# A decoder layer in which GpSimd computes the low halves of the out projection's weights in place of VectorE

## The reference

```
x = layernorm(x + attention(x))          # 16 query heads, 4 key/value heads of 128, rotary,
                                         # causal windows of 128 queries x 256 keys
x = layernorm(x + cross(x, ctx))         # softmax over ctx's own energies, applied to x
x = layernorm(x + moe(x))                # 2 shared and 16 routed experts, top 4, width 176

# the end of attention, with out_kernel of shape (16 * 128, 256):
out = ob.reshape(b, t, H * D)
return jnp.dot(out, out_kernel)
```

## Time and profile before

| | |
|---|---|
| Median of three runs | 456.1 us (454.03 to 456.33) |
| Span of the profiled execution | 457.5 us, its own time beside the runs |
| PE (TensorE matmul) | 406.4 us busy, 89% |
| PEld (weight load) | 343.3 us, 75% |
| DVE (VectorE) | 308.9 us, 68% |
| ACT (ScalarE) | 267.0 us, 58% |
| POOL (GpSimd) | 168.3 us, 37% |
| Mean granted TensorE clock | 0.960 of full speed |

### The profile page before, as it was taken

The page is one execution under the profiler, slowest core; times in us unless marked ns, Lnnn a source line. Parts: engine busy times, 40 slices in busy tenths (PEclk is TensorE's granted clock), DMA queues, the critical chain, the costliest instruction groups (busy, mean ns, idle before and its releaser), DMA issues.

```text
span 457.5 us, 8275 instructions
## 1 busy us (share of the span) xinstructions
PE 406.4 (89%) x2297; PEld 343.3 (75%) x2297; DVE 308.9 (68%) x851; ACT 267.0 (58%) x659; POOL 168.3 (37%) x288
## 2 busy tenths in 40 slices
PE   3977898999889999899998896884899999999992
PEld 2766787999779988789997674561788888888871
DVE  1685999797987889887889745440655555555545
ACT  3566977785657775567774631610655555555553
POOL 0142656553664556535646402010222232222210
PEclk9986999999999999999999996997799999999997
DMA  6511230000000000000002950035433333333302
GB/s 225 198 47 47 91 116 25 3 0 2 1 1 23 0 0 0 0 0 0 0 0 60 327 183 0 0 44 99 113 92 95 100 96 91 96 100 94 90 10 92
DMA packets 20716, 29.29 MB, mean 64 GB/s; under 512 B 1305, under 2 KB 15794, under 8 KB 20696
## 3 DMA queue, kind: packets, MB, share of 16 engines
q1 hardware_dynamic: 20696, 29.05, 22.9%
HBM read 27.19 MB, written 1.86 MB: 63 GB/s over the span
## 4 chain that ended last, share of the span: by engine, by line
PE 67%; DVE 16%; issue 7%; DMA 4%; ACT 2%; POOL 2%; SPq 1%; POOLq 0%; DVEq 0%; ACTq 0%
PE bank L524 18%; PE bank L525 17%; PE bank L526 17%; PE bank L608 4%; PE bank L617 2%; PE bank L580 2%; PE bank L607 2%; DMA gates_d<-gatesT 2%; DMA gate_rows<-gates_d 1%; DVE by_sin L1047 1%; DVE by_cos L1046 1%; PE bank L574 1%; DVE scores L1057 1%; DVE xln L1118 1%; PE bank L680 1%
## 5 line engine op out<-in xcount | busy, mean ns | idle before, releaser
L1002 DVE TENSOR_TENSOR hid<-hid,gate_rows 128x512 f32<-128x512 f32 (+1 forms) x46 | 32.0, 699 | 68.8 <-ACT hid L810 50.8
L810 ACT ACTIVATE hid<-bank,b_cols 128x512 f32<-128x512 f32 (+1 forms) x50 | 34.3, 687 | 42.1 <-PE bank L526 42.1
L1286 POOL TENSOR_SCALAR nprobs<-probs,rsums 128x128 f32<-128x128 f32 x64 | 24.0, 375 | 91.6 <-DVE rsums L1064 86.2
L1293 POOL TENSOR_TENSOR w_lo<-w_raw,w_hi 128x256 fp32r<-128x256 f32 (+1 forms) x25 | 20.7, 829 | 89.6 <-ACT w_hi L802 89.6
L1278 POOL TENSOR_TENSOR queryT<-by_cos,by_sin 128x512 f32<-128x512 f32 x32 | 42.5, 1328 | 28.8 <-DVE by_sin L1047 27.8
L524 PE MATMUL bank<-hid_hi,w_hi 128*128 128x512 f32 (+1 forms) x100 | 40.1, 401 | 8.2 <-DVE hid_lo L989 8.0
L989 DVE TENSOR_TENSOR hid_lo<-hid,hid_hi 128x512 fp32r<-128x512 f32 (+1 forms) x50 | 39.3, 819 | 5.7 <-ACT hid_hi L819 3.1
L870 ACT COPY swapped<-bank 64x512 f32<-64x512 f32 x40 | 23.3, 583 | 32.6 <-PE bank L526 32.4
L524 PE MATMUL bank<-x2T_hi,w_hi 128*128 128x512 f32 (+1 forms) x100 | 40.5, 405 | 0.5 <-DVE xln L1031 0.5
L524 PE MATMUL bank<-xT_hi,wq_hi 128*128 128x256 f32 x128 | 38.8, 303 | 1.7 <-issue 1.2
L525 PE MATMUL bank<-x2T_lo,w_hi 128*128 128x512 f32 (+1 forms) x100 | 40.1, 401 | 0.0
(11 more groups left out here) (174 smaller groups left out, 1176.5 us busy)
## 6 DMA issues: line engine op xcount, KB each, us to landing
gate_rows<-gates_d SPq DMA_DIRECT2D x22, 512.0 KB
w_raw<-in_L_ffn_routed_w SPq DMA_DIRECT2D x2, 1408.0 KB, 8.2
w_raw<-in_L_ffn_routed_w SPq DMA_DIRECT2D x1, 2688.0 KB, 12.5
stage<-in_L_attn_q_kernel SPq DMA_DIRECT2D x4, 512.0 KB, 6.3
stage<-in_L_attn_out_kernel SPq DMA_DIRECT2D x4, 512.0 KB, 3.5
xb<-in_x SPq DMA_DIRECT2D x4, 256.0 KB, 2.9
res<-in_x SPq DMA_DIRECT2D x1, 1024.0 KB, 6.2
out<-x SPq DMA_DIRECT2D x8, 128.0 KB, 1.8
```

The costliest lines, as they stand in the source:

```text
L810: nc.scalar.activation(hid[0:n, par, h * HALF:(h + 1) * HALF], bank[2 + 2 * par + h][0:n, :], ACT.Relu, bias=b1_cols[0:n, bass.ds(c, 1)]). ...
L1002: nc.vector.tensor_tensor(hid[0:n, par, cols], hid[0:n, par, cols], gate_rows[0:n, par, cols], ALU.mult).then_inc(gated, 1)
L1286: nc.gpsimd.tensor_scalar(nprobs[:, u, 0:W], probs[:, u, 0:W], rsums[:, u, 0:1], 1.0, ALU.mult, ALU.mult)
```

## The change

`POOL_PIECES` names o0 to o3. `window_order` now gives GpSimd an order with the once-only work too: a piece of `POOL_PIECES` goes to GpSimd, the others stay on VectorE, all at the same places of `PIECE_AT`. GpSimd gets a function `once`, which waits for ScalarE's high half and subtracts, and signals a semaphore of its own, `w_lo_pool`. Those who waited for `w_lo` to count a piece of the out projection now wait for `w_lo_pool` (`project_out` on TensorE, the slot "y" on ScalarE, which keeps its wait for the others as well). The second branch of SyncE's wait is never taken: the last load, piece 9, waits for piece 5, which is VectorE's.

With the places of `PIECE_AT`, GpSimd's order in the first sequence becomes: normalise 6, o0, q5, normalise 7, q6, o1, normalise 8, normalise 9, o2, normalise 10, q7, normalise 11, o3, normalise 12.

```diff
@@ -108,6 +108,8 @@
 
 PIECE_NAMES = ["q0", "k", "q1", "q2", "v", "q3", "o0", "o1", "o2", "o3"]
 PIECE_AT = dict(zip(PIECE_NAMES, (-2.1, -2.05, -0.9, 2.2, 3.1, 5.4, 6.6, 8.1, 10.1, 12.1)))
+POOL_PIECES = PIECE_NAMES[6:]
+DVE_PIECES = 6
 ONCE_AT = {
     "pe": {"ctx turned": -2.4, "ctx projected": -2, "energy 0": -0.9, "energy 1": -0.85,
            "energy 2": 0.2, "energy 3": 0.25, "attT 0": 1.1, "attT 1": 1.15, "attT 2": 2.1,
@@ -137,8 +139,9 @@
     turns = [(in_window(at)[1], in_window(at)[0], work, of) for at, work, of in events]
     assert all(window in (0, 1) for _, window, _, _ in turns), engine
     turns += [(at, "once", name, 0) for name, at in ONCE_AT[engine].items()]
-    if engine in ("act", "dve"):
-        turns += [(at, "once", "piece", PIECE_NAMES.index(name)) for name, at in PIECE_AT.items()]
+    if engine != "pe":
+        turns += [(at, "once", "piece", PIECE_NAMES.index(name)) for name, at in PIECE_AT.items()
+                  if engine == "act" or (name in POOL_PIECES) == (engine == "pool")]
     return [(window, work, of) for _, window, work, of in sorted(turns, key=lambda e: e[0])]
 
 
@@ -338,7 +341,7 @@
         ld_ident, ld_tables, ld_res = sem("ld_ident"), sem("ld_tables"), sem("ld_res")
         ld_xb = sem("ld_xb")
         ld_stage = [sem(f"ld_stage{i}") for i in range(4)]
-        w_hi, w_lo = sem("w_hi"), sem("w_lo")
+        w_hi, w_lo, w_lo_pool = sem("w_hi"), sem("w_lo"), sem("w_lo_pool")
         projected, emptied = sem("projected"), sem("emptied")
         swap_done, rope_mul, rope_add = sem("swap_done"), sem("rope_mul"), sem("rope_add")
         split_hi = sem("split_hi")
@@ -452,7 +455,10 @@
             for n in range(4, len(PIECES)):
                 if n == 6:
                     small_loads()
-                sp.wait_ge(w_lo, n - 3)
+                if n - 4 < DVE_PIECES:
+                    sp.wait_ge(w_lo, n - 3)
+                else:
+                    sp.wait_ge(w_lo_pool, n - 3 - DVE_PIECES)
                 sp.dma_start(stage_view(n), PIECES[n][0]).then_inc(ld_stage[n % 4], 16)
             sp.dma_start(res[:], x_tiles).then_inc(ld_res, 16)
 
@@ -639,7 +645,7 @@
                     after("dve", "centT_lo")
                 if g == 0 and blk == 0:
                     e.wait_ge(res_done, b + 1)
-                e.wait_ge(w_lo, piece_count(f"o{g}"))
+                e.wait_ge(w_lo_pool, g + 1)
                 e.wait_ge(oT_done, pv_count(b, g, blk))
                 for a in range(G):
                     q = slice(a * W, (a + 1) * W)
@@ -850,7 +856,8 @@
                 if kind == "x":
                     nc.scalar.copy(xT_hi[:, j, :], o[:, 0:T]).then_inc(split_hi, 1)
                 elif kind == "y":
-                    e.wait_ge(w_lo, len(PIECES))
+                    e.wait_ge(w_lo, DVE_PIECES)
+                    e.wait_ge(w_lo_pool, len(PIECES) - DVE_PIECES)
                     e.sem_inc(act_passed, 1)
                     nc.scalar.copy(x2T_hi[:, :, bass.ds(b * T, T)],
                                    o[:].rearrange("p (k t) -> p k t", k=KC)).then_inc(x2_hi_done, 1)
@@ -1288,6 +1295,11 @@
                                         ALU.mult, ALU.mult).then_inc(norm_done, 1)
 
 
+            def once(_, n):
+                e.wait_ge(w_hi, n + 1)
+                nc.gpsimd.tensor_tensor(PIECES[n][2], stage_view(n), PIECES[n][1].bitcast(F32),
+                                        ALU.subtract).then_inc(w_lo_pool, 1)
+
             def low_w1(c, par, n=P):
                 e.wait_ge(w1_hi_done, c + 1)
                 nc.gpsimd.tensor_tensor(w1_lo[:, par, :, 0:n], w1_raw[:, :, bass.ds(c * P, n)],
@@ -1330,9 +1342,9 @@
 
             for s in (norm_done, turned):
                 e.sem_inc(s, AHEAD)
-            doers = {"slot": slot, "normalise": normalise, "norm 1": lambda b, _: layer_norm(b, 0),
+            doers = {"slot": slot, "normalise": normalise, "once": once, "norm 1": lambda b, _: layer_norm(b, 0),
                      "norm 2": lambda b, _: layer_norm(b, 1)}
-            take_turn("pool", 0, (0,), doers)
+            take_turn("pool", 0, (0, "once"), doers)
             with e.Fori(1, B) as b:
                 take_turn("pool", b, (0, 1), doers)
             take_turn("pool", B, (1,), doers)
```

## The result

The changed kernel took 459.98 us at the median of 18 runs (456.36 to 462.02), beside 456.38 for the kernel before on the same chip: a ratio of **1.0078, 95% interval [1.0055, 1.0100]**, 2.5 to 4.6 us slower. Two more sets of the same kernel gave 1.0059 [1.0025, 1.0094] and 1.0106 [1.0065, 1.0146]. The forecast was 457.0 and its likeliest case was "within 0.5%"; that was wrong.

The account below looks back on a forecast made before the run. VectorE looked limiting over 57 to 79 us, with TensorE's idle time capping any gain. Turn 8's +2.2 us less idle 0.84 and 0.45 gave +0.9 us on the 456.1 median: 457.0 us, range 454.3 to 460.4.

Parts of the forecast that it names:

- within 0.5%: Whole kernel: time changes by less than 2.3 us either way, chance 0.60.
- the ceiling: TensorE's listed idle, 57.5 to 79 us: even an infinitely fast VectorE gains at most about 1.6 us (1.57 idle).
- The cost of one subtraction: Each 128x1024 piece on GpSimd: 2.38 us, extrapolated from 256 and 512 columns; ends 1.26 and 2.92.
- GpSimd's queue: Ahead of TensorE's turn 8, first sequence: two pieces of 2.38 us delay normalise 8, making turn 8 2.2 us late.
- The holds: VectorE instructions behind a GpSimd piece wait for its end: by_sin 5 some 2.6 us, an ntop near 2 us.
- the replay: Instruction-by-instruction re-timing of the first sequence from 57.6 us; puts sequence 1's query product 0.9 us late, at 79.34.
- The tie: At o3: o3 (76.59) and ntop 13 (76.60) nearly coincide; if o3 wins, ntop 13 is held to 78.97; chance 0.22.
- The first rival: o3 holds ntop 13, so sequence 1's query product comes at 80.9 us; +2.5 us, 458.6 on the median, chance 0.22.
- rival 2: TensorE's granted clock falls behind 1.9 us idle ahead of turn 8; up to +4.3 us, 460.4 on the median, chance 0.18.
- The third rival: GpSimd's subtraction lets by_sin 5 through, so only GpSimd's own order counts; -1.2 us, 454.9 on the median, chance 0.18.
- the stated range: Whole kernel: total time predicted between 454.3 and 460.4 us.

Follow-up runs that it names:

- The version with two of the four pieces hidden: Kernel before, all pieces on VectorE, subtractions o0 and o1 moved early into VectorE's idle stretch at 40 to 44 us; ratio 0.9961.
- The run that writes without reading: Changed kernel with each GpSimd subtraction replaced by three zero fills of the low half, which read nothing; ratio 1.0015.
- halves: Changed kernel with each GpSimd subtraction split into two instructions of 512 columns; ratio 1.0036.
- o3 alone: Changed kernel with only subtraction o3 on GpSimd, o0 to o2 staying on VectorE; ratio 1.0035.

## Why the prediction was right and wrong

**What bounds the kernel, and the ceiling.** Right as a reading of place: the 3.8 us that the chain shows on wo_lo were no measure of the gain. But the ceiling was too low. The version with two of the four pieces hidden gained 1.74 us of distance, with 0.45 of the listed idle still there, where the ceiling had been 1.57 for all four. It had counted only the idle stretches that the records list, and these start at a matmul's modelled end. From start to start more was lost: behind the values product turn 7 came 0.57 us sooner in the version with two pieces early (0.28 listed), turn 10 another 1.00 behind turn 8 (0.84 listed).

**The cost of one subtraction.** Right. 2.38 us estimated, measured (the stage tile's GpSimd instruction, columns as in the earlier trace rows):

```profile
L1300 POOL TENSOR_TENSOR wo_lo<-stage,wo_hi x4: 2361/2386/2396, 57.9 to 75.7; 128x1024 fp32r<-128x1024 f32 x4
```

**GpSimd's queue and turn 8.** The size is right, the cause only in part. From the values product to turn 8 it is 10.71 us before (67.77 - 57.06) and 12.81 after (68.94 - 56.13): 2.1 us late, 2.2 predicted. The prediction called this GpSimd's queue, with two pieces in it. But behind o0 GpSimd stood idle, for by_sin 5 and for the reciprocal of head 7:

```profile
60.86 1.28 POOL L1285 TENSOR_TENSOR queryT<-by_cos,by_sin 128x512 f32<-128x512 f32 x1 [0.63 <-DVE by_sin L1054]
...
63.67 0.37 POOL L1293 TENSOR_SCALAR nprobs<-probs,rsums 128x128 f32<-128x128 f32 x1 [1.52 <-DVE rsums L1071]
```

That reciprocal, before and after:

```profile
63.07 0.15 DVE L1064 RECIPROCAL rsums<-psums 128x2 f32<-128x2 f32 x1
...
63.28 0.15 DVE L1071 RECIPROCAL rsums<-psums 128x2 f32<-128x2 f32 x1
```

It comes 6.01 us behind the values product before and 7.15 after. So 1.1 of the 2.1 us come by o0's hold of by_sin 5, through VectorE, and only the other 1.0 by o1 in GpSimd's own queue. The run that writes without reading agrees: with by_sin 5 free, turn 8 was sooner although the queue was longer. Later places agree too: the input transposes were forecast 20.70 us behind the values product and came 20.57 behind it (76.70 - 56.13).

**The holds.** Right in kind, and by_sin 5 in size (2.65 us; about 2.6 predicted). The Trainium skill (SBUF — State Buffer, "Who interferes with whom") says that the loser waits for the whole instruction, and that a VectorE instruction with two SBUF inputs meets only GpSimd instructions that read. Both agree with the runs: holds end with the GpSimd instruction, halves of 512 columns halve them, and behind a fill by_sin took 0.68 us. ntop 10 lasted less than expected (0.65 us, where the prediction looked for near 2), and by_sin 7 was hardly held (0.79 us), since o1 and o2 were nearly over.

**A wait that the replay missed.** TensorE's second values product waited 1.05 us for oT_lo (61.53), for its result goes to the same PSUM bank (`pv_bank`) that oT_lo reads; oT_lo stood behind the held by_sin 5. It cost nothing, as turn 8 was later still: 1.05 us are spent here and 1.29 at turn 8, less the 0.28 that turn 7 no longer waits, and that makes the 2.1.

**The tie, the step that failed.** The prediction had o3 at 76.59 and ntop 13 at 76.60 and gave VectorE the better chance, on one row: a normalise recorded at 71.51 had lost to a by_sin recorded at 71.56. Where the late one was an ntop, the earlier record won every time that it was seen: 64.46 against 64.47, 75.65 against 75.67, 74.37 against 74.38 with o3 alone. The row that the prediction leaned on has a by_sin in that place, and it repeats: with o3 alone a normalise of 70.72 took 1.00 us and a by_sin of 70.78 its clean 0.68. That the normalise was a second part directly behind a first does not explain it, for in the changed kernel such a second part (69.20) did hold ntop 11 (69.21, 0.50 us). Why it lost to by_sin stays open. The rule of the Trainium skill (SBUF — State Buffer, "Who interferes with whom"), by which the one that issues first holds the other, agrees with the three pairs of recorded starts, and on recorded starts not with these two. What the tie cost is shown from two sides: 1.55 us by moving o3 behind normalise 12, and 1.0 us by giving it to GpSimd alone. The first rival had +2.5 us; the distance says +2.42.

**The clock, rival 2.** It did not happen in the three profiles of the changed kernel (idle 1.27 to 1.29 us ahead of turn 8, where I had 1.9), and it did behind 1.88 and 2.06 us in two of the edited kernels (halves, and writing without reading), in executions whose clock had stayed at 1.00 over 28 to 46 us. Which of the two, the longer idle stretch or the earlier clock, makes the difference is not shown. There it cost 1.55 us from turn 8 to turn 9, not 3.4.

**From 2.4 to 3.6 us.** Open in part. Each run lists its mean granted clock. Among runs at 0.978 the median span is 452.5 before (11 runs) and 454.8 after (2 runs), and at 0.967 it is 455.1 (22) and 457.65 (4): +2.3 and +2.55, as the distance says. At 0.964, the largest group, it is 456.1 (34) and 459.85 (14): +3.75. The shortest spans differ by 2.5 us (452.0 and 454.5) and the longest by 3.0 (457.7 and 460.7), but long ones are more frequent: 19 of 36 executions of the changed kernel reach 459.4 us, and only 13 of 110 of the kernel before reach 457.0, which is 2.4 less. So the median moved further than the distance.

One of the long ones was profiled, the changed kernel's second. The five profiles of the two kernels, cut at the same places:

| kernel | to the values product | distance | to the end of the attention | behind it | span | mean clock |
|---|---|---|---|---|---|---|
| before | 57.06 | 21.34 | 184.42 | 194.7 | 457.5 | 0.960 |
| before, again | 54.27 | 21.35 | 184.36 | 192.6 | 452.6 | 0.978 |
| changed | 56.13 | 23.76 | 184.45 | 193.6 | 457.9 | 0.967 |
| changed, again | 56.72 | 23.74 | 184.42 | 195.5 | 460.4 | 0.957 |
| changed, a third time | 56.17 | 23.74 | 184.44 | 192.9 | 457.3 | 0.968 |

In the long one the clock was 1.00 from 48 to 262 us, behind turn 8 too, and what it has above the other two lies ahead of the values product and in the feed-forward layer, where the change touches nothing. Two stages of its profile:

```profile
48.00:262.00 214.00, 199.62 (x1373) 180.12 (x1372) 184.72 (x591) 144.95 (x411) 121.52 (x224) 1.00 0.10 30
280.00:300.00 20.00, 16.85 (x61) 11.67 (x60) 9.30 (x41) 8.49 (x14) 0.88 (x3) 0.74 0.00 0
```

The clock of 0.74 over 280 to 300 us was 0.83 and 0.91 in the other two. So the middle stages give 2.4 us in every profile, and from profile to profile the time ahead of them varies by up to 2.8 us and the time behind the attention by up to 2.9. Why the changed kernel should meet the long kind more often, no run shows; a fall behind turn 8 in executions that were not profiled is not excluded either. A loss of 2.4 us would be a ratio of 1.0053: the second set's interval holds it, the first set's begins just above it and the third's at 1.0065. That the time lies inside the stated range is therefore in part luck: the queue, the holds and the tie together gave 2.4 of the 3.6 us, and the rest is none of the things that the prediction had summed.

**The third rival** (VectorE held less, -1.2 us) is excluded by every profile of the changed kernel: by_sin 5 lasts 2.64 or 2.65 us in all three.

## What to carry to other kernels

An engine taken off the chain by giving its work to a second one gains only if the second neither stands in front of the next wait nor shares something with the first: here 5.1 us of VectorE's work became 9.5 us of GpSimd's, and VectorE stayed busy for 20.25 of 22 us, some 6 of them held up. Look first for an idle stretch of the engine that already does the work: two pieces moved by 20 us on the same engine gave 0.4%, and four moved to another cost 0.8%. And where two chains that start at one instruction meet within a few hundredths of a microsecond, work out both outcomes and move one of them by a place; here the earlier record won against every ntop, but not against by_sin.

## What the runs showed of the hardware

- A VectorE instruction of two elements a partition (ntop) takes 0.17 us alone, and up to 2.39 us behind a GpSimd subtraction that started 0.02 us earlier. GpSimd fills, which read nothing, hold it too (0.78 and 0.94 us), but not a product of two SBUF operands (0.68 us), which a subtraction holds for up to 2.65 us.
- Splitting GpSimd's instruction in two costs it about 0.15 us (2.53 against 2.38) and halves the longest hold (1.30 against 2.39).
- The kernel before has executions with and without a fall of TensorE's clock over 28 to 46 us; its profiled spans were 457.5 us with it and 452.6 without (mean clock 0.960 and 0.978). Of these 4.9 us, 2.8 lie ahead of the values product and 2.1 behind the attention, a spread wider than the change.
- TensorE's clock fell to 1.2 GHz (0.50 over 68 to 70 us) behind idle stretches of 1.88 and 2.06 us in two profiles, and not behind 1.27 to 1.29 us in three; from turn 8 to turn 9 it cost 1.55 us.
